# The first graph layer's scan: gate product moved from VectorE to GpSimd, same-row marks in PSUM

## The chip, the cores and the metric

The kernel runs on one core of a Trainium2 chip. The metric is the device time of one execution in microseconds (us), given as the median of several runs. Engines are called as in the profile: PE is TensorE, DVE is VectorE, ACT is ScalarE, POOL is GpSimd, SP is SyncE, the last of which only issues DMAs here. L829 is line 829 of the kernel before.

## What is computed

A graph network of two layers over 6250 nodes of 64 features and 206250 edges, each with a source `src`, a destination `dst`, a type and 32 attributes. The change lies in the first layer, which is this part of the reference:

```python
edge_index = jnp.stack([src, dst])
h = jnp.maximum(_layernorm(x, axis=-1), 0.0)
head = entity_emb[edge_index[0]]                      # entity_emb = h
tail = entity_emb[edge_index[1]]
rel = relation_emb[edge_type]
att_scores = jax.nn.sigmoid(jnp.concatenate([head, rel], axis=-1) @ att_w + att_b)
neighbor_emb = att_scores * tail
aggr_emb = jax.ops.segment_sum(neighbor_emb, edge_index[0], num_segments=N_ENTITIES)
x = x + jnp.tanh(aggr_emb @ W_w.T + W_b)
```

So every edge gives its destination's features times one gate, and the products are summed by source. The second layer is an attention over the same edges, and its result goes through a linear map and is added to `x`.

## The kernel before, in words

Everything runs on one core, in stages one after the other; a stage is an `nc.Block()` (item 1 below has two) in which each engine has its own program, and the engines meet only by semaphores.

1. `setup` and `histogram` load the inputs, normalise the nodes and count the edges of each source.
2. `sort` writes a record of 100 floats for each edge (32 attributes, destination, source, gate, a pad, and the destination's 64 features) into an HBM table in the order of the sources, by scatters from POOL.
3. `relation_layer` is the first layer's scan, the stage of the change.
4. `relation_nodes` takes the running sums at the last edge of each source, and computes the node update and the tables for the second layer.
5. `attention_layer` is the second layer's scan. For each chunk POOL issues 26 gathers (L1126) and DVE does products (L1254, L1256, L1274, L1277), a reduce (L1257) and scans (L1241, L1286).
6. `attention_nodes` writes the result.

The sorted records are cut so that each of the 128 partitions holds a run of 1612 consecutive records. `relation_layer` walks these runs in 62 chunks of T = 26 records per partition, 31 turns of a loop with two halves (b = 0 and 1, buffers of the same number); chunk n = 2i + b. `loop` writes the first and last turn out and loops over the 29 between. The sums by source are made by one scan over the 64 features x 27 places of a chunk, state = keep x state + add: `keep` is 1 where a record has the same source as the one before it, and `add` is the gated features. Place 0 of each feature holds the sum carried over from the chunk before, with keep 0.

Per chunk the engines do this:

- **SP** (L753) loads `rec_r` with the records, 1300 KB, into one of two buffers, once the product two chunks back is done (`s_add`).
- **DVE** prepares (`prepare`, L809 to L812): three small copies out of the records (destination as index, destination, source) and a compare of neighbouring sources into `same`, all 26 wide. Then `scan`: the carry copy (L822), the gate product (L823: features transposed to feature-major times the gate, 1664 elements, into the one buffer `add_r`), and the scan (L829, 1728 elements).
- **ACT** spreads `same` over the 64 features into `keep_r` (L778), copies the scan's result back to record order into `packed_r` (L790) and issues its store (L792, 832 KB).
- **POOL** does nothing here. There is a second way for unsorted extremes (`gather` true, chosen at run time by the flag `k.slow`), in which POOL gathers the destinations' features (L766). In this input the flag is 0, and the trace has no instruction on `got_r`.

The order of the work is the order of each engine's program as written; DVE prepares chunk n right before its product when nothing is gathered:

```python
for b in range(2):
    n = 2 * i + b
    if not gather:
        prepare(n, i, b)
    elif not at_end(i, b):
        prepare(n + 1, i + b, 1 - b)
    scan(n, i, b, gather)
```

Of the kernel before, what the change touches and what calls it, by code (L numbers as in the profile page):

```python
# [22 lines left out]
P = 128  # L23
N, D, E, EC = 6250, 64, 206250, 32
# [6 lines left out]
T = 26  # L31
# [8 lines left out]
T1 = T + 1  # L40
# [29 lines left out]
def bc(ap, dim, n):  # L70

    a = ap.unsqueeze(dim)
    shape = list(a.shape)
    shape[dim] = n
    return a.broadcast_to(shape)


def wait(eng, s, n):

    if not isinstance(n, int) or n > 0:  # L80
        eng.wait_ge(s, n)


def loop(eng, body):


    body(0)
    with eng.Fori(1, PAIRS - 1) as i:
        body(i)
    body(PAIRS - 1)  # L90
# [54 lines left out]
def at_start(i, b=0):  # L145
    return isinstance(i, int) and i == 0 and b == 0


def at_end(i, b=1):
    return isinstance(i, int) and i == PAIRS - 1 and b == 1  # L150
# [568 lines left out]
def relation_layer(k):  # L719


    nc = k.nc
    with ExitStack() as ctx:
        tile, bank, sem = helpers(k, ctx)
        rows = tile("rows", [P, 1 + NT])
        rec = [tile(f"rec_r{b}", [P, T, REC]) for b in range(2)]
        idx = [tile(f"idx_r{b}", [P, T], I32) for b in range(2)]
        got = [tile(f"got_r{b}", [P, T, D]) for b in range(2)]

        keep = [tile(f"keep_r{b}", [P, D, T1]) for b in range(2)]  # L730
        add = tile("add_r", [P, D, T1])
        state = [tile(f"state_r{b}", [P, D, T1]) for b in range(2)]
        packed = [tile(f"packed_r{b}", [P, T, D]) for b in range(2)]
        s_zero, s_idx, s_add, s_state, s_keep, s_packed, s_dve, s_passed = (
            sem(n) for n in ("s_zero_r", "s_idx_r", "s_add_r", "s_state_r", "s_keep_r", "s_packed_r", "s_dve_r", "s_passed_r"))
        s_rec, s_got, s_store = ([sem(f"{n}{b}") for b in range(2)] for n in ("s_rec_r", "s_got_r", "s_store_r"))
        records_v, sums_v = by_run(k.records), by_run(k.sums0)

        def either(eng, body):

            flag = eng.value_load(k.slow[0:1, 0:1], min_val=0, max_val=CHUNKS)
            with eng.If(flag != 0):
                body(True)
            with eng.Else():
                body(False)

        with nc.Block() as block:  # L747
            @block.sync
            def _(sp):
                def body(i):  # L750
                    for b in range(2):
                        wait(sp, s_add, 2 * i + b - 1)
                        sp.dma_start(rec[b][:], records_v[:, bass.ds(i * 2 * T + b * T, T), :]).then_inc(s_rec[b], 16)  # L753

                loop(sp, body)

            @block.gpsimd
            def _(pool):
                def body(i):
                    for b in range(2):  # L760
                        n = 2 * i + b
                        wait(pool, s_add, n - 1)
                        pool.wait_ge(s_idx, n + 1)
                        pool.sem_inc(s_passed, 1)
                        for t in range(T):
                            nc.gpsimd.indirect_dma_start(  # L766
                                got[b][:, t, :], None, k.h_table,
                                bass.IndirectOffsetOnAxis(ap=idx[b][:, t:t + 1], axis=0)).then_inc(s_got[b], 16)

                either(pool, lambda gather: loop(pool, body) if gather else pool.sem_inc(s_passed, 1))  # L770

            @block.scalar
            def _(act):
                def mark(n, i, b):

                    act.wait_ge(s_idx, n + 1)
                    wait(act, s_state, n - 1)
                    nc.scalar.copy(keep[b][:, :, 1:T1], bc(k.same[:, bass.ds(n * T, T)], 1, D)).then_inc(s_keep, 1)  # L778

                act.wait_ge(s_zero, 4)  # L780
                mark(0, 0, 0)

                def body(i):
                    for b in range(2):
                        n = 2 * i + b
                        if not at_end(i, b):
                            mark(n + 1, i + b, 1 - b)
                        act.wait_ge(s_state, n + 1)
                        wait(act, s_store[b], 16 * i)
                        nc.scalar.copy(packed[b][:], state[b][:, :, 1:T1].rearrange("p d t -> p t d")).then_inc(s_packed, 1)  # L790
                        act.wait_ge(s_packed, n + 1)
                        act.dma_start(sums_v[:, bass.ds(n * T, T), :], packed[b][:]).then_inc(s_store[b], 16)  # L792

                loop(act, body)
                for b in range(2):
                    act.wait_ge(s_store[b], 16 * PAIRS)

            @block.vector
            def _(dve):
                c = Chain(dve, s_dve, 2 * 4)  # L800

                def prepare(n, i, b):

                    t0 = i * 2 * T + b * T
                    dve.wait_ge(s_rec[b], 16 * (i + 1))
                    if at_start(i, b):

                        c.mark(nc.vector.tensor_copy(rows[:, 0:1], rec[b][:, 0:1, SRC]))
                    c.mark(nc.vector.tensor_copy(idx[b][:], rec[b][:, :, DST]))  # L809
                    c.mark(nc.vector.tensor_copy(k.dst_s[:, bass.ds(t0, T)], rec[b][:, :, DST]))  # L810
                    c.then(nc.vector.tensor_copy(rows[:, bass.ds(t0 + 1, T)], rec[b][:, :, SRC]))
                    nc.vector.tensor_tensor(k.same[:, bass.ds(t0, T)], rows[:, bass.ds(t0 + 1, T)],  # L812
                                            rows[:, bass.ds(t0, T)], ALU.is_equal).then_inc(s_idx, 1)

                def scan(n, i, b, gather):
                    if gather:
                        dve.wait_ge(s_got[b], SCATTERED * (i + 1))
                    h_dst = got[b][:] if gather else rec[b][:, :, H0:REC]
                    if at_start(i, b):
                        c.mark(nc.vector.memset(add[:, :, 0:1], 0.0))  # L820
                    else:
                        c.mark(nc.vector.tensor_copy(add[:, :, 0:1], state[1 - b][:, :, T:T1]))  # L822
                    nc.vector.tensor_tensor(add[:, :, 1:T1], h_dst.rearrange("p t d -> p d t"),  # L823
                                            bc(rec[b][:, :, GATE], 1, D), ALU.mult).then_inc(s_add, 1)
                    c.wait()
                    dve.wait_ge(s_add, n + 1)
                    dve.wait_ge(s_keep, n + 1)
                    wait(dve, s_packed, n - 1)
                    nc.vector.tensor_tensor_scan(state[b][:].rearrange("p d t -> p (d t)"), keep[b][:].rearrange("p d t -> p (d t)"),  # L829
                                                 add[:].rearrange("p d t -> p (d t)"), 0.0, ALU.mult, ALU.add).then_inc(s_state, 1)  # L830
                    dve.wait_ge(s_state, n + 1)

                for b in range(2):
                    nc.vector.memset(keep[b][:, :, 0:1], 0.0).then_inc(s_zero, 2)

                def way(gather):
                    c.begin(0)
                    c.fewer = 0
                    if gather:
                        prepare(0, 0, 0)  # L840

                    def body(i):
                        if not at_start(i):
                            c.begin(i)
                        for b in range(2):
                            n = 2 * i + b
                            if not gather:
                                prepare(n, i, b)
                            elif not at_end(i, b):
                                prepare(n + 1, i + b, 1 - b)  # L850
                            scan(n, i, b, gather)
                        if not at_end(i):
                            c.end()

                    loop(dve, body)

                either(dve, way)
                c.wait()
                c.mark(nc.vector.tensor_copy(k.first_row[:], rows[:, 1:2]))
                c.mark(nc.vector.tensor_copy(k.last_row[:], rows[:, NT:NT + 1]))  # L860
                c.then(nc.vector.tensor_copy(k.tail0[:], state[1][:, :, T]))
# [785 lines left out]
```

## Time and profile before

| What | Value |
|---|---|
| Median of 3 runs | 7819.6 us (7811.6 to 7821.93) |
| Span of the profiled execution, first to last instruction | 6240.3 us |
| Its own time | the profile gives no other than the span; 1579.3 us below the median |
| Busy in the span | DVE 65%, POOL 67%, PE 39%, ACT 36% |
| Stage of `relation_layer` | 2452.4 to 2962.5 us |

The profile is taken in one execution. "Busy" is time inside instructions; issuing DMAs and waiting for semaphores is not busy. In a group of instructions stand the line, the engine, the operation, output and inputs, the count, the busy time and mean of one, and then the idle time of the engine before them with what ended it. The page's own list of the costliest groups is led by the indirect DMAs of POOL in `attention_layer` and `sort`; the groups of `relation_layer` are found by asking for its stretch of time.

### The profile page before, as it was taken

Reading aid. Unit: us, or ns where it says so; the run is one execution under the profiler, and the core shown is the slowest. Engines: PE = TensorE matmul, PEld = TensorE weight load, DVE = VectorE, ACT = ScalarE, POOL = GpSimd, SP = SyncE. Lnnn points to the kernel's source line nnn. Section 1 sums busy time; section 2 is a strip of 40 time slices with the busy share of each in tenths; the row PEclk is TensorE's granted clock in tenths of the full one; section 3 lists DMA queues with packets and bytes.
Section 4 is the critical chain, followed back from the end, with each engine's and each line's share of the span. In section 5 each row is a group of like instructions: output and inputs, shape, how many; then the busy total and the mean of one; then the engine's idle time right before and its main releaser. Section 6 shows DMA issues by size and latency. Waiting matters only on the chain. (4 is left out here: it accounts for less than half of the span.)

```text
span 6240.3 us, 79656 instructions
## 1 busy us (share of the span) xinstructions
PE 2457.8 (39%) x26472; PEld 2145.9 (34%) x26472; DVE 4084.2 (65%) x6681; ACT 2268.7 (36%) x3099; POOL 4166.8 (67%) x3385
## 2 busy tenths in 40 slices
PE   2877666666666660000632222222222222222215
PEld 2876666666666660000421111111111111111115
DVE  6987777777777773999345655655655655655654
ACT  0033333333333332666244344344344344344332
POOL 0067777777777775000568888888888888888863
PEclk9987777777777775555555555555555555555555
DMA  4022222222222222777133233233233233233211
GB/s 57 18 79 83 74 84 74 84 80 77 83 74 84 74 81 98 271 269 256 39 97 92 81 85 91 80 85 90 80 85 91 80 86 90 80 87 89 80 54 22
DMA packets 459619, 572.09 MB, mean 92 GB/s; under 512 B 349939, under 2 KB 358003, under 8 KB 451632
## 3 DMA queue, kind: packets, MB, share of 16 engines
q1 hardware_dynamic: 309440, 265.27, 15.5%
q0 software_dynamic: 107904, 193.55, 10.9%
q10 hardware_dynamic: 42224, 112.63, 4.7%
q8 instruction: 27, 0.44, 0.0%
q14 instruction: 24, 0.20, 0.0%
HBM read 308.06 MB, written 263.14 MB: 92 GB/s over the span
## 5 line engine op out<-in xcount | busy, mean ns | idle before, releaser
L1126 POOL DMA_INDIRECT got_a<-kv_table,idx_a x1612 | 2390.6, 1483 | 501.1 <-issue 491.0
L497 POOL DMA_INDIRECT records<-rec,place x1612 | 1620.6, 1005 | 824.9 <-issue 491.2
L1254 DVE TENSOR_TENSOR prod<-got_a,query 128x1664 f32<-128x1664 f32 x62 | 188.8, 3046 | 1123.9 <-DMA got_a<-kv_table,idx_a 1123.9
L1140 PE MATMUL p_a<-ident,flat_attr 128*128 128x128 f32 x434 | 108.0, 426 | 1778.2 <-ACT flat_attr L1174 1778.2
L1140 PEld LDWEIGHTS p_a<-ident,flat_attr 128*128 128x128 f32 x434 | 83.5, 221 | 1790.6 <-ACT flat_attr L1174 1790.6
L518 PE MATMUL p_look<-parts,lo_hot_t 128*128 128x98 bf16 x4836 | 503.8, 240 | 129.9 <-DVE earlier L703 129.8
L609 ACT COPY lo_hot_t<-p_t 128x512 bf16<-128x512 bf16 x434 | 241.1, 556 | 711.6 <-PE p_t L542 700.2
L703 DVE TENSOR_TENSOR earlier<-p_same,less_b 128x512 bf16<-128x512 f32 x434 | 282.4, 651 | 274.7 <-PE p_same L564 269.6
L685 DVE TENSOR_SCALAR dst_hot<-p_dst,number 128x512 bf16<-128x512 f32 x434 | 309.0, 712 | 215.1 <-PE p_dst L552 213.8
L518 PEld LDWEIGHTS p_look<-parts,lo_hot_t 128*128 128x128 bf16 x4836 | 397.8, 116 | 140.6 <-DVE earlier L703 140.5
L1198 ACT COPY packed_a<-state_a 128x1768 f32<-128x1768 f32 x62 | 228.0, 3678 | 534.7 <-DVE state_a L1286 534.7
L521 PE MATMUL p_look<-hi_hot,earlier 128*128 128x49 bf16 x1612 | 400.5, 248 | 0.0
L1151 PE MATMUL p_w<-w_t,relu 128*128 128x128 f32 x868 | 261.5, 400 | 352.0 <-ACT soft L1187 352.0
L1151 PEld LDWEIGHTS p_w<-w_t,relu 128*128 128x128 f32 x868 | 214.1, 303 | 421.9 <-ACT soft L1187 421.9
L917 POOL IOTA hi_at_i<- 128x49 int32 x1 | 0.2, 170 | 518.2 <-POOLq L747 518.2
L580 ACT COPY h_dst<-p_h 128x256 f32<-128x256 f32 x434 | 156.1, 360 | 517.4 <-PE p_h L529 514.6
L568 PE MATMUL p_place<-hi_hot,lo_hot 128*128 128x49 bf16 x1612 | 231.0, 274 | 272.7 <-DVE parts L695 272.6
L638 DVE TENSOR_TENSOR picked<-p_look,hi_hot 128x392 f32<-128x392 f32 x434 | 336.6, 776 | 0.0
L1192 ACT ACTIVATE add_a<-below_a 128x104 f32<-128x104 f32 x62 | 18.0, 290 | 781.1 <-DVE below_a L1271 781.1
L564 PE MATMUL p_same<-lo_hot_t 128*128 128x128 bf16 x1612 | 189.3, 247 | 247.0 <-ACT lo_hot_t L609 247.0
L520 PE MATMUL p_look<-hist,lo_hot_t 128*128 128x49 bf16 x2294 | 285.8, 206 | 0.0
L529 PE MATMUL p_h<-window,dst_hot 128*128 128x64 bf16 x4836 | 267.9, 214 | 0.0
(307 smaller groups left out, 8628.9 us busy)
## 6 DMA issues: line engine op xcount, KB each, us to landing
rec_r<-records SPq DMA_DIRECT2D x62, 1300.0 KB, 6.5
sums<-packed_a ACTq DMA_DIRECT2D x62, 936.0 KB, 3.7
q_starts<-zero_q SPq DMA_DIRECT2D x62, 884.0 KB
qin<-q_starts SPq DMA_DIRECT2D x62, 884.0 KB, 6.9
sums<-packed_r ACTq DMA_DIRECT2D x62, 832.0 KB, 6.6
records<-rec,place POOLq DMA_INDIRECT x1612
attr_a<-records SPq DMA_DIRECT2D x62, 416.0 KB, 5.0
got_a<-kv_table,idx_a POOLq DMA_INDIRECT x1612, 2.6
```

What stands on the lines that cost most here:

```text
L497: nc.gpsimd.indirect_dma_start(k.records, bass.IndirectOffsetOnAxis(ap=place[b][:, t:t + 1], axis=0), rec[b][:, t, :], None).then_inc(s_se ...
L518: nc.tensor.matmul(both, at, k.parts[qb][:, part, :, :], start=(part == 0), stop=False)
L520: nc.tensor.matmul(to, at, hist[qb][:, e, :], start=False, stop=False)
L521: last = nc.tensor.matmul(to, earlier[qb][:, j, :], k.hi_hot[b][:, :, g * G + j], start=False, stop=True)
L529: last = nc.tensor.matmul(p_h[:, j * D:(j + 1) * D], dst_hot[qb][:, j * P:(j + 1) * P], window[b][:, part, :], start=(part == 0), stop=(pa ...
L568: last = nc.tensor.matmul(p_place[:, 0:HI], k.lo_hot[b][:, :, t], k.hi_hot[b][:, :, t], start=False, stop=True, skip_group_check=True)
L609: nc.scalar.copy(lo_hot_t[qb][:, 0:size(g) * P], p_t[:, 0:size(g) * P]).then_inc(s_t_copied, 1)
L638: nc.vector.tensor_tensor(picked[:, 0:n, :, :], p_look[gb][:, 0:n * 2 * HI].rearrange("p (g a h) -> p g a h", a=2, h=HI), bc(k.hi_hot[b][: ...
L685: nc.vector.tensor_scalar(dst_hot[qb][:, 0:m * P], p_dst[:, 0:m * P], k.number[:], None, ALU.is_equal).then_inc(s_dst_hot, 1)
L703: nc.vector.tensor_tensor(earlier[qb][:, 0:m, :], p_same[:, 0:m * P].rearrange("p (g e) -> p g e", e=P), bc(k.less_b[:], 1, m), ALU.mult). ...
L1126: nc.gpsimd.indirect_dma_start(got[b][:, t, :], None, k.kv_table, bass.IndirectOffsetOnAxis(ap=idx[b][:, t:t + 1], axis=0)).then_inc(s_got ...
L1151: nc.tensor.matmul(to, relu[:, g * P:(g + 1) * P], k.w2_t[:], start=True, stop=False)
```

## The change

The gate product becomes an instruction of POOL and writes one of two `add_r` buffers. `keep_r` moves from SBUF to PSUM, four banks for each buffer. DVE prepares chunk n + 1 before it scans chunk n in both ways, so it has one loop in place of two. The carry copy gets a semaphore of its own, and SP's load waits also for the compare (`s_idx`) of the chunk two back. POOL's product waits for the records of its chunk and for the scan two chunks back, which read the same `add_r` buffer. What is computed stays the same. The core of the diff:

```diff
-        keep = [tile(f"keep_r{b}", [P, D, T1]) for b in range(2)]
-        add = tile("add_r", [P, D, T1])
+        add = [tile(f"add_r{b}", [P, D, T1]) for b in range(2)]
...
+        keep_flat = [ctx.enter_context(nc.psum_tensor(f"keep_r{b}", [P, 4 * 512], F32))[:, 0:D * T1] for b in range(2)]
+        keep = [flat.rearrange("p (d t) -> p d t", t=T1) for flat in keep_flat]
...
                     for b in range(2):
                         wait(sp, s_add, 2 * i + b - 1)
+                        wait(sp, s_idx, 2 * i + b - 1)
                         sp.dma_start(rec[b][:], records_v[:, bass.ds(i * 2 * T + b * T, T), :]).then_inc(s_rec[b], 16)
...
+                def weigh(n, i, b, gather):
+
+                    pool.wait_ge(s_rec[b], 16 * (i + 1))
+                    if gather:
+                        pool.wait_ge(s_got[b], SCATTERED * (i + 1))
+                    wait(pool, s_state, n - 1)
+                    h_dst = got[b][:] if gather else rec[b][:, :, H0:REC]
+                    nc.gpsimd.tensor_tensor(add[b][:, :, 1:T1], h_dst.rearrange("p t d -> p d t"),
+                                            bc(rec[b][:, :, GATE], 1, D), ALU.mult).then_inc(s_add, 1)
+
+                def way(gather):
+                    if gather:
+                        fetch(0, 0)
+
+                    def body(i):
+                        for b in range(2):
+                            n = 2 * i + b
+                            if gather and not at_end(i, b):
+                                fetch(n + 1, 1 - b)
+                            weigh(n, i, b, gather)
+
+                    loop(pool, body)
+
+                either(pool, way)
...
-                        c.mark(nc.vector.tensor_copy(add[:, :, 0:1], state[1 - b][:, :, T:T1]))
-                    nc.vector.tensor_tensor(add[:, :, 1:T1], h_dst.rearrange("p t d -> p d t"),
-                                            bc(rec[b][:, :, GATE], 1, D), ALU.mult).then_inc(s_add, 1)
-                    c.wait()
+                        nc.vector.tensor_copy(add[b][:, :, 0:1], state[1 - b][:, :, T:T1]).then_inc(s_carry, 1)
+                    dve.wait_ge(s_carry, n + 1)
                     dve.wait_ge(s_add, n + 1)
                     dve.wait_ge(s_keep, n + 1)
                     wait(dve, s_packed, n - 1)
-                    nc.vector.tensor_tensor_scan(state[b][:].rearrange("p d t -> p (d t)"), keep[b][:].rearrange("p d t -> p (d t)"),
-                                                 add[:].rearrange("p d t -> p (d t)"), 0.0, ALU.mult, ALU.add).then_inc(s_state, 1)
+                    nc.vector.tensor_tensor_scan(state[b][:].rearrange("p d t -> p (d t)"), keep_flat[b],
+                                                 add[b][:].rearrange("p d t -> p (d t)"), 0.0, ALU.mult, ALU.add).then_inc(s_state, 1)
                     dve.wait_ge(s_state, n + 1)
...
+                c.begin(0)
+                prepare(0, 0, 0)
+
+                def body(i):
+                    if not at_start(i):
+                        c.begin(i)
+                    for b in range(2):
+                        n = 2 * i + b
+                        if not at_end(i, b):
+                            prepare(n + 1, i + b, 1 - b)
+                        scan(n, i, b)
+                    if not at_end(i):
+                        c.end()
+
+                loop(dve, body)
```

How this moves instructions is seen on DVE and POOL. First DVE in the changed kernel, the first half of a turn of the loop in `relation_layer` (`same` is the compare of chunk n + 1, the copy into `add_r` is the carry of chunk n, `SCALAR_TENSOR_TENSOR` is the scan of chunk n; `ISA` and `REGISTER_ALU` rows are loop counting and waits):

```order
L832 CAST idx_r<-rec_r 128x26 [waits s_rec_r1]
L833 ISA
L833 COPY dst_s<-rec_r 128x26
L834 ISA
L834 COPY rows<-rec_r 128x26
L108 ISA
L835 ISA [waits s_dve_r]
L835 TENSOR_TENSOR same<-rows 128x26
L842 COPY add_r<-state_r 128x64
L843 REGISTER_ALU
L81 REGISTER_ALU [waits s_keep_r,s_add_r,s_carry_r]
L847 SCALAR_TENSOR_TENSOR state_r<-keep_r,add_r 128x1728 [waits s_packed_r]
```

Before, the product stood between the carry copy and the scan, on DVE; now the preparing of the next chunk, the carry copy and the scan follow one another, and the scan waits for POOL (`s_add_r`).

Then POOL in the changed kernel, the way without gathers in `relation_layer`, which before held one branch and no work (first turn, loop, last turn):

```order
L777 TENSOR_TENSOR add_r<-rec_r 128x64x26 [waits s_rec_r0]
L777 TENSOR_TENSOR add_r<-rec_r 128x64x26 [waits s_rec_r1]
L88 UNCONDITIONAL_BRANCH
L88 ISA
L81 ISA [waits s_rec_r0]
L777 TENSOR_TENSOR add_r<-rec_r 128x64x26 [waits s_state_r]
L777 TENSOR_TENSOR add_r<-rec_r 128x64x26 [waits s_state_r,s_rec_r1]
L88 REGISTER_ALU
L88 COMPARE_AND_BRANCH
L777 TENSOR_TENSOR add_r<-rec_r 128x64x26 [waits s_state_r,s_rec_r0]
L777 TENSOR_TENSOR add_r<-rec_r 128x64x26 [waits s_state_r,s_rec_r1]
```

The first two products wait for their records alone; each later one waits for its records and for the scan of two chunks before.

## Rows read from the trace of the kernel before

**Rows 1.** The page's head: the span, then busy time and share per engine.

```profile
span 6240.3 us, 79656 instructions
...
PE 2457.8 (39%) x26472; PEld 2145.9 (34%) x26472; DVE 4084.2 (65%) x6681; ACT 2268.7 (36%) x3099; POOL 4166.8 (67%) x3385
```

**Rows 2.** Busy time of each engine in the stage, then clock, DMA share, GB/s.

```profile
2452.40:2962.50 510.10, 0.00 (x0) 0.00 (x0) 471.55 (x440) 307.49 (x124) 0.00 (x0) 0.50 0.77 264
```

**Rows 3.** Groups of instructions by line in the stage, DVE and ACT.

```profile
L829 DVE TENSOR_TENSOR_SCAN state_r<-keep_r,add_r 128x1728 f32<-128x1728 f32 x62 | 233.0, 3758 | 4.9
...
L823 DVE TENSOR_TENSOR add_r<-rec_r 128x1664 f32<-128x1664 f32 x62 | 196.0, 3162 | 0.0
...
L790 ACT COPY packed_r<-state_r 128x1664 f32<-128x1664 f32 x62 | 215.2, 3471 | 2.1 <-DVE state_r L829 2.1
L778 ACT COPY keep_r<-same 128x1664 f32 (+1 forms) x62 | 98.1, 1582 | 266.1 <-DVE same L812 266.1
```

**Rows 4.** Timeline of DVE over one chunk: start us, us, instruction, idle before.

```profile
2481.44 0.18 DVE L809 CAST idx_r<-rec_r 128x26 int32<-128x26 f32 x1
...
2481.70 0.18 DVE L811 COPY rows<-rec_r 128x26 f32 x1
2482.03 0.19 DVE L812 TENSOR_TENSOR same<-rows  x1
2482.13 0.22 DVE L822 COPY add_r<-state_r 128x64 f32<-128x64 f32 x1
...
2485.45 3.76 DVE L829 TENSOR_TENSOR_SCAN state_r<-keep_r,add_r 128x1728 f32<-128x1728 f32 x1
2489.77 0.18 DVE L809 CAST idx_r<-rec_r 128x26 int32<-128x26 f32 x1 [0.56 <-DVE state_r L829]
```

**Rows 5.** Timeline of DVE: the first and the last index copy.

```profile
2458.16 0.17 DVE L809 CAST idx_r<-rec_r 128x26 int32<-128x26 f32 x1
...
2950.94 0.18 DVE L809 CAST idx_r<-rec_r 128x26 int32<-128x26 f32 x1
```

**Rows 6.** DMA from 2452 to 2965: SP's queue, and the loads' time to landing.

```profile
q1 hardware_dynamic: 8928, 82.54, 52.2%
...
rec_r<-records SPq DMA_DIRECT2D x62, 1300.0 KB, 6.5
```

**Rows 7.** Timeline of POOL at the program's start.

```profile
0.30 0.10 POOL L1638 MEMSET const-float32-0.0<- 128x1 f32 x1 [0.30 <-issue]
...
1.81 0.29 POOL L273 TENSOR_SCALAR_AFFINE_SELECT ident<-ident 128x128 f32<-128x128 f32 x1 [0.16 <-POOL ones L271]
```

**Rows 8.** Groups of DVE over the whole span: one PSUM input, dense SBUF inputs.

```profile
L703 DVE TENSOR_TENSOR earlier<-p_same,less_b 128x512 bf16<-128x512 f32 x434 | 282.4, 651 | 274.7 <-PE p_same L564 269.6 <-issue 0.2
...
L128 DVE TENSOR_TENSOR big<-h 128x3136 f32<-128x3136 f32 x1 | 3.4, 3425 | 0.0
```

**Rows 9.** Timeline: POOL's gathers beside DVE, in `relation_nodes` and `attention_layer`.

```profile
2970.90 6.69 DVE L1029 TENSOR_TENSOR own<-iota_p,own_at 128x6272 f32<-128x6272 f32 x1
2971.87 6.53 POOL L920 DMA_INDIRECT sums_n<-sums,last_at  x1 [0.30 <-issue]
...
4003.80 3.70 DVE L1274 TENSOR_TENSOR got_a<-got_a,net 128x1664 f32<-128x1664 f32 x1
...
4005.01 3.24 POOL L1126 DMA_INDIRECT got_a<-kv_table,idx_a  x1 [0.30 <-issue]
...
4007.60 3.00 DVE L1277 TENSOR_TENSOR add_a<-got_a,add_a 128x1664 f32<-128x1664 f32 x1
...
4010.87 3.98 DVE L1286 TENSOR_TENSOR_SCAN state_a<-scale,add_a 128x1836 f32<-128x1836 f32 x1
4011.69 3.92 POOL L1126 DMA_INDIRECT got_a<-kv_table,idx_a  x1 [0.30 <-issue]
...
4045.70 3.25 DVE L1257 TENSOR_REDUCE logit_a<-prod 128x104 f32<-128x1664 f32 x1
4046.79 0.94 POOL L1126 DMA_INDIRECT got_a<-kv_table,idx_a  x1 [0.30 <-issue]
```

More of the change, by code:

```diff
@@ L728, in relation_layer @@
         got = [tile(f"got_r{b}", [P, T, D]) for b in range(2)]
-        keep = [tile(f"keep_r{b}", [P, D, T1]) for b in range(2)]
-        add = tile("add_r", [P, D, T1])
+        add = [tile(f"add_r{b}", [P, D, T1]) for b in range(2)]
         state = [tile(f"state_r{b}", [P, D, T1]) for b in range(2)]
         packed = [tile(f"packed_r{b}", [P, T, D]) for b in range(2)]
-        s_zero, s_idx, s_add, s_state, s_keep, s_packed, s_dve, s_passed = (
-            sem(n) for n in ("s_zero_r", "s_idx_r", "s_add_r", "s_state_r", "s_keep_r", "s_packed_r", "s_dve_r", "s_passed_r"))
+        keep_flat = [ctx.enter_context(nc.psum_tensor(f"keep_r{b}", [P, 4 * 512], F32))[:, 0:D * T1] for b in range(2)]
+        keep = [flat.rearrange("p (d t) -> p d t", t=T1) for flat in keep_flat]
+        s_zero, s_idx, s_add, s_carry, s_state, s_keep, s_packed, s_dve, s_passed = (
+            sem(n) for n in ("s_zero_r", "s_idx_r", "s_add_r", "s_carry_r", "s_state_r", "s_keep_r", "s_packed_r", "s_dve_r", "s_passed_r"))
         s_rec, s_got, s_store = ([sem(f"{n}{b}") for b in range(2)] for n in ("s_rec_r", "s_got_r", "s_store_r"))
@@ L758, in _, with fetch @@
             def _(pool):
[L759 to L770, printed above, removed]
+                def fetch(n, b):
+                    wait(pool, s_add, n - 1)
+                    pool.wait_ge(s_idx, n + 1)
+                    pool.sem_inc(s_passed, 1)
+                    for t in range(T):
+                        nc.gpsimd.indirect_dma_start(
+                            got[b][:, t, :], None, k.h_table,
+                            bass.IndirectOffsetOnAxis(ap=idx[b][:, t:t + 1], axis=0)).then_inc(s_got[b], 16)
+                def weigh(n, i, b, gather):
[17 more added lines that the diff above has]
+                either(pool, way)
             @block.scalar
@@ L799, in _ @@
             def _(dve):
-                c = Chain(dve, s_dve, 2 * 4)
+                c = Chain(dve, s_dve, 2 * 3)
                 def prepare(n, i, b):
@@ L813, in prepare, with scan @@
                                             rows[:, bass.ds(t0, T)], ALU.is_equal).then_inc(s_idx, 1)
[L815 to L818, printed above, removed]
+                def scan(n, i, b):
                     if at_start(i, b):
-                        c.mark(nc.vector.memset(add[:, :, 0:1], 0.0))
+                        nc.vector.memset(add[b][:, :, 0:1], 0.0).then_inc(s_carry, 1)
                     else:
-                        c.mark(nc.vector.tensor_copy(add[:, :, 0:1], state[1 - b][:, :, T:T1]))
-                    nc.vector.tensor_tensor(add[:, :, 1:T1], h_dst.rearrange("p t d -> p d t"),
-                                            bc(rec[b][:, :, GATE], 1, D), ALU.mult).then_inc(s_add, 1)
-                    c.wait()
+                        nc.vector.tensor_copy(add[b][:, :, 0:1], state[1 - b][:, :, T:T1]).then_inc(s_carry, 1)
+                    dve.wait_ge(s_carry, n + 1)
                     dve.wait_ge(s_add, n + 1)
@@ L834, in _ @@
                     nc.vector.memset(keep[b][:, :, 0:1], 0.0).then_inc(s_zero, 2)
[L836 to L857, printed above, removed]
+                c.begin(0)
[11 more added lines that the diff above has]
+                loop(dve, body)
                 c.wait()
```

## The prediction

> **What bounds the kernel now.** I went from the whole to the stage, then to one chunk. The page's first lines say that no engine is full over the span: DVE 65%, POOL 67%, DMA light [rows 1]. So the change must be priced in its own stage. The table by stage gives the first layer's scan 510.1 us, with DVE busy 471.55 of them, ACT 307.49, POOL nothing, and the DMA engines busy 0.77 of the time [rows 2]. The groups of DVE there show why: 62 chunks, each a product of 3162 ns and a scan of 3758 ns, and, in the timeline, five small instructions of 0.18 to 0.22 us [rows 3, 4]. They stand end to end, with holes of 0.03 to 0.56 us between chunks [rows 4]. From the first index copy at 2458.16 to the last at 2950.94 are 61 chunks, so a chunk takes 8.08 us [rows 5]. The idle time in the groups agrees: ACT sat 266.1 us until DVE's compare [rows 3]. DVE alone sets the pace. Behind it stand the DMA engines: 0.77 x 510.1 / 62 = 6.34 us per chunk.
>
> **The change, part by part.** The sum is against the profiled execution, whose span is 6240.3 us; the median of the runs, 7819.6, is 1579.3 us more. I take what lies around the span as unchanged and add the difference in the stage to the median.
>
> *The product leaves DVE.* Gone: 62 x 3.16 = 196 us of DVE. What stays per chunk is 8.08 - 3.16 = 4.92 us: four instructions of preparing, the carry copy, the scan, the gaps.
>
> *The product arrives on POOL,* and no row has such an instruction. Its price P is bounded by rows. From below: POOL's select over 128 elements takes 0.29 us, and a one-element fill 0.10 [rows 7], so 1.5 ns an element with one input read, or 2.6 us for 1664. With two inputs read in turn the same slope gives 5.0 us. From above: both inputs here are strided by a record of 400 bytes. DVE needs 1.8 ns an element for this product ((3162 - 150) / 1664) and 1.04 for a dense one (3425 ns for 3136, [rows 8]), a surcharge of 0.76 ns; added to 5.0 it gives 6.3. ACT's strided copy takes 3471 ns [rows 3]; two such streams, less one fixed part, are 6.6. I take P = 5.6, between POOL's own slope and the surcharge, and keep 2.6 to 6.6. The Trainium skill, "GPSIMD Engine Reference", section 3.1, states 4497 ns for a GpSimd add of 2048 elements; in proportion that is an estimate of 3.65 us here, and by its section 7 (steps over 8 bytes cost about half again) 5.5 us.
>
> *Does it run beside DVE?* This decides the sign. The rows show a lock in one direction. DVE's product of two SBUF inputs of 6.69 us at 2970.90 stretched POOL's gather at 2971.87 to 6.53 us, that is until 0.8 us after DVE's end. In the second layer the gather at 4011.69 lasted 3.92 us, again until 0.8 us after a two-input scan; the one at 4046.79, under a reduce with one input, took 0.94 [rows 9]. The scan with its marks in PSUM has one SBUF input, like that reduce, so I let it run beside POOL. But preparing still has a compare of two SBUF inputs, `same`, and it stands before the scan in every chunk. Note also the gather of 4005.01: it ended at 4008.25, though the next two-input product had begun at 4007.60, 0.1 us after the first, so POOL got in between the two [rows 9]. Now the order. POOL's product of chunk n+1 and DVE's preparing of n+1 wait for the same two things, the load of n+1 and the end of scan n-1. They start together. POOL reacts in 0.16 us [rows 7]; preparing and carry take from 2481.44 to 2482.35, 0.9 us, with a hole before `same` [rows 4]. POOL gets in. If the lock holds the other way too, DVE's compare then stands until the product ends, the carry and scan n stand behind it, and POOL may not start n+2 before scan n is done, as it writes the buffer that this scan reads. So they alternate:
>
> chunk = 4.92 (DVE) + 0.15 (POOL's reaction) + 5.6 (P) = 10.67 us; change = 62 x (10.67 - 8.08) = +161 us.
>
> The reverse direction is not in these rows, since no POOL instruction there reads SBUF for long. The Trainium skill, "SBUF — State Buffer", "Who interferes with whom", states it: such a pair excludes each other for the whole instruction, and issue order decides who blocks. By that rule the sum stands; without it, it is the first rival's.
>
> *Marks in PSUM.* ACT's copy of 1582 ns may change by some 0.1 us either way; ACT has 8.08 - 3.47 - 1.58 = 3.0 us to spare per chunk [rows 3]. The scan takes (3758 - 158) / 1728 = 2.08 ns an element; DVE's product with one PSUM input takes 651 ns for 512 [rows 8], about 1 ns an element, so I expect no loss. If the read were added it would be 1.8 us x 62 = 111 us more; that far end I hold for unlikely.
>
> *Preparing ahead* only shifts the same instructions, except at the start: `same` of chunk 1 now precedes the first scan and waits for the second load. A load costs 52.2% of 513 us / 62 = 4.3 us of the engines [rows 6], so it lands that much after the first, past the 3.16 us of the first product; with the compare behind it, +2 us. SP's added wait for s_idx is for a compare that lies before the scan of the product it waits for anyway: nothing. If POOL is late, SP's loads are late by the same; at 10.67 us a load of 6.5 us [rows 6] is hidden.
>
> Sum: 161 + 2 = 163; 7819.6 + 163 = **7983 us**.
>
> **The rivals.**
>
> *1. No exclusion against the small instructions (faster).* Then POOL's product lies under the scan. Candidates per chunk: POOL 5.75; DVE 4.92; ACT 5.05 and its DMA issue; the buffer ring (6.5 landing + 5.6 + 0.3) / 2 = 6.2; DMA 6.34. I take 6.5: 62 x (6.5 - 8.08) = -98, so 7722 us. For it: no row shows POOL holding DVE. Against: the lock seen from the other side. It decides wherever DVE's compare and copies pass while POOL reads.
>
> *2. DVE often wins the race.* After a chunk whose preparing is through before POOL begins, the product hides. Half the chunks each way: (10.67 + 6.5) / 2 = 8.6, +32 us, 7852. Against it: POOL's 0.16 us against 0.9 us of preparing.
>
> *3. Excluded, but the product is short.* Break-even is P = 3.16 - 0.15 = 3.0 us; at the low bound of 2.6 the change gives 62 x (2.6 - 3.0) = -25, 7795. That needs the second input to be free.
>
> *4. Side by side, but POOL is the bound.* If P were 10 us, outside my bounds, the chunk is 10.2 and the time 7950.
>
> **How the numbers follow.** Alternation 0.53, rival 1 0.31, rival 2 0.09, rival 3 0.03, rival 4 0.04. The likeliest gives 7983, and alone, for P of 4.3 to 6.6, it gives 7900 to 8045. A measurement of this kernel tells about 0.2%, 16 us, from no change. Faster: rival 1 but for a slow product (0.29), and the fast ends of rivals 2 and 3 (0.04): 0.33. Same: the middle of rival 2 (0.04) and the alternation with P near 3 (0.02): 0.06. Slower: the rest, 0.61. The range must reach rival 1 at 7722; I take 7715 to 8045.
>
> **What would show it.** Right: in the stage of the first scan, POOL busy for some 62 x 5.6 = 350 us; the stage about 670 us long; on DVE the compare `same`, or the copy before it, stretched or begun late by 5 us in each chunk, and no overlap of POOL's product with it; the DMA share down to 0.58; the scan still 3758 ns. Wrong: small instructions at 0.18 us while POOL's product runs and a stage near 415 us with a DMA share of 0.95 (rival 1); a POOL product under 3 us; a scan longer than 3.9 us; or a stage whose chunks differ in length in turn (rival 2). Other stages should keep their length.

## The result, and the profile after

The changed kernel takes 7998.7 us (median of 4 runs, 7993.0 to 8001.29) against 7820.8 us before (4 runs, 7811.6 to 7825.84). The ratio is 1.0228, with a 95% interval of 1.0214 to 1.0243: 178 us slower, where +163 was forecast.

First a correction that the reading of all numbers needs. The profile of the kernel before has a span of 6240.3 us, the one of the changed kernel 7991.1. The difference is not the change. In the view by stages, up to the scan's stage 2452 us passed in the one and 3937 in the other, with the same code. The kernel before, profiled once more (the first experiment), took 6239.34 us with a span of 6237.4, so only 2 us lie around a span. I had put the 1579 us between span and median around the span. They lie in the stages before the scan, where the two traces differ by 1484 us, and for 90 us behind it. So I compare medians only within one set of runs, and in the traces the stage itself, from the first load of `rec_r` to the first instruction of the next stage. That stage was 513.6 us in both profiles of the kernel before, and is 690.2 us in the changed one: +176.6 us, all of the difference.

The stage of the changed kernel, busy time of each engine, then clock, DMA share and GB/s (it answers to [rows 2]):

```profile
3936.80:4627.00 690.20, 0.00 (x0) 0.00 (x0) 648.99 (x378) 312.38 (x124) 390.78 (x63) 0.50 0.52 196
```

DVE is "busy" for 648.99 us, though it lost 196 us of work. What that is shows in the groups by line, busy and mean, then idle before with its releaser ([rows 3]):

```profile
L777 POOL TENSOR_TENSOR add_r<-rec_r 128x1664 f32<-128x1664 f32 x62 | 390.8, 6303 | 288.2 <-DVE state_r L847 277.7 <-DMA rec_r<-records 10.5
L832 DVE CAST idx_r<-rec_r 128x26 int32<-128x26 f32 x62 | 359.7, 5802 | 15.8 <-DVE state_r L847 11.9
L847 DVE TENSOR_TENSOR_SCAN state_r<-keep_r,add_r 128x1728 f32<-128x1728 f32 x62 | 232.9, 3757 | 4.7
...
L801 ACT COPY keep_r<-same 128x1664 f32 (+1 forms) x62 | 96.1, 1550 | 269.1 <-DVE same L835 269.1
L833 DVE CAST dst_s<-rec_r 128x26 f32 (+1 forms) x62 | 28.7, 463 | 0.0
L835 DVE TENSOR_TENSOR same<-rows (+1 forms) x62 | 17.5, 282 | 8.2
```

The index copy of 26 numbers, 182 ns before, now has a mean of 5802 ns. The product on POOL takes 6303 ns, and POOL sat idle 277.7 us until scans had ended. The timeline over two chunks shows how these fit ([rows 4]; start, us, instruction, idle before):

```profile
3999.30 3.76 DVE L847 TENSOR_TENSOR_SCAN state_r<-keep_r,add_r 128x1728 f32<-128x1728 f32 x1
4003.14 6.31 POOL L777 TENSOR_TENSOR add_r<-rec_r 128x1664 f32<-128x1664 f32 x1 [4.66 <-DVE state_r L847]
...
4003.19 6.29 DVE L832 CAST idx_r<-rec_r 128x26 int32<-128x26 f32 x1
...
4009.40 0.17 DVE L833 CAST dst_s<-rec_r 128x26 f32 x1
4009.49 0.17 DVE L834 COPY rows<-rec_r 128x26 f32 x1
4009.80 0.19 DVE L835 TENSOR_TENSOR same<-rows  x1
4009.91 0.22 DVE L842 COPY add_r<-state_r 128x64 f32<-128x64 f32 x1
...
4010.16 3.76 DVE L847 TENSOR_TENSOR_SCAN state_r<-keep_r,add_r 128x1728 f32<-128x1728 f32 x1
```

The scan ends, POOL's product starts first by 0.05 us, DVE's index copy starts and stands until the product is over, then the other small instructions run at their usual 0.17 to 0.22 us, and the scan follows. Product and scan alternate: in the whole stage no scan overlaps a product. The first chunks show that it isn't a matter of this one copy. There POOL came later into the row, and the compare and the next copy were held instead:

```profile
3942.67 12.58 POOL L777 TENSOR_TENSOR add_r<-rec_r 128x1664 f32<-128x1664 f32 x2 [10.48 <-DMA rec_r<-records]
3942.70 0.17 DVE L834 COPY rows<-rec_r 128x26 f32<-128x26 f32 x1
3942.91 6.13 DVE L835 TENSOR_TENSOR same<-rows 128x26 f32<-128x26 f32 x1
...
3949.05 6.24 DVE L833 CAST dst_s<-rec_r 128x26 int32<-128x26 f32 x1
...
3955.77 3.76 DVE L847 TENSOR_TENSOR_SCAN state_r<-keep_r,add_r 128x1728 f32<-128x1728 f32 x1
```

Of the 60 later products, 58 hold the index copy, for 6.05 to 6.31 us. In the two others the index copy started up to 0.05 us before the product and took 0.18 us, and the copy after it was held instead. So it did not help DVE to be first with a small instruction.

From the first index copy at 3942.52 to the last at 4604.87 are 61 chunks of 10.86 us ([rows 5]: 8.08). Forecast was 10.67.

### The profile page after: what moved, and what is told of

The parts are those of the page before. It is cut to its first block and busy times, and to the rows that moved or that the text cites. A ratio compares the mean times of both kernels' runs of the same rounds, so it can differ in the third digit from the quotient of the medians.

```text
span 7991.1 us, 79829 instructions
## 1 busy us (share of the span) xinstructions
PE 2703.3 (34%) x26472; PEld 2243.8 (28%) x26472; DVE 4265.7 (53%) x6619; ACT 2274.5 (28%) x3099; POOL 4496.2 (56%) x3447
## 5 line engine op out<-in xcount | busy, mean ns | idle before, releaser
L497 POOL DMA_INDIRECT records<-rec,place x1612 | 1558.0, 966 | 2371.9 <-ACTq L599 1887.7
L518 PE MATMUL p_look<-parts,lo_hot_t 128*128 128x98 bf16 x4836 | 528.3, 249 | 417.2 <-DVE earlier L703 407.1
L529 PE MATMUL p_h<-window,dst_hot 128*128 128x64 bf16 x4836 | 369.2, 218 | 576.0 <-issue 576.0
L777 POOL TENSOR_TENSOR add_r<-rec_r 128x1664 f32<-128x1664 f32 x62 | 390.8, 6303 | 288.2 <-DVE state_r L847 277.7
L529 PEld LDWEIGHTS p_h<-window,dst_hot 128*128 128x128 bf16 x4836 | 273.9, 114 | 589.5 <-issue 589.5
L568 PE MATMUL p_place<-hi_hot,lo_hot 128*128 128x49 bf16 x1612 | 255.8, 273 | 440.6 <-issue 227.7
L564 PE MATMUL p_same<-lo_hot_t 128*128 128x128 bf16 x1612 | 233.3, 256 | 435.3 <-issue 435.1
L832 DVE CAST idx_r<-rec_r 128x26 int32<-128x26 f32 x62 | 359.7, 5802 | 15.8 <-DVE state_r L847 11.9
```

The source lines that it names most:

```text
L497: nc.gpsimd.indirect_dma_start(k.records, bass.IndirectOffsetOnAxis(ap=place[b][:, t:t + 1], axis=0), rec[b][:, t, :], None).then_inc(s_se ...
L518: nc.tensor.matmul(both, at, k.parts[qb][:, part, :, :], start=(part == 0), stop=False)
L529: last = nc.tensor.matmul(p_h[:, j * D:(j + 1) * D], dst_hot[qb][:, j * P:(j + 1) * P], window[b][:, part, :], start=(part == 0), stop=(pa ...
L568: last = nc.tensor.matmul(p_place[:, 0:HI], k.lo_hot[b][:, :, t], k.hi_hot[b][:, :, t], start=False, stop=True, skip_group_check=True)
L777: nc.gpsimd.tensor_tensor(add[b][:, :, 1:T1], h_dst.rearrange("p t d -> p d t"), bc(rec[b][:, :, GATE], 1, D), ALU.mult).then_inc(s_add, 1)
```

## The experiments

The theory, called exclusion below: while POOL's product reads SBUF, DVE's small copies and its compare cannot run; the scan is free of it only because its marks are in PSUM, and with the marks in SBUF product and scan would hold each other. The rivals: the two engines run side by side and the loss lies in the later order of work (preparing ahead); PSUM; or the product's length alone. "Chunk" below is the time between the first and the last index copy over 61.

**The kernel before, again.**

> The kernel before, unchanged, for a second profile: its first one has a span 1579 us under the median, the changed kernel's has one of 7991. Expected: a span near 7818 us, with the difference in the sorting stage, and the first layer's scan stage again 513 us long (8.08 us a chunk). If the difference lay around the span, the span would be 6240 again.

6239.34 us, span 6237.4, stage 513.7, chunk 8.08. The stage is as long as expected. The span is not near 7818, as I had expected: time and span agree within 2 us, and the whole run took the short time. In another set of runs, with experiments of its own below, the kernel before took 7853.5 us. Below, each kernel is compared with the kernel before as run in the same set. Variants of both kernels appear at either level, so the two levels, short and long, are not of the kernel, and the scan's stage keeps its length: 513.6 us here, and 512.5 at the long level with the marks alone moved to PSUM. Each set of runs was on one chip: the short level was seen on chips 0 and 3, the long one on chip 12, and for the first result the chip is not known. In the profile of the changed kernel PE sat idle 576.0 us before the matmuls of L529 with no releaser that the profile shows ("issue"), in the first profile of the kernel before 0.0. Whether the chip sets the level, or something else, wasn't tried.

**The product's start moved behind the small instructions.**

```diff
-                    wait(pool, s_state, n - 1)
+                    wait(pool, s_carry, n)
```

> Changed kernel, but POOL's product of chunk n+1 waits for the carry copy of chunk n instead of the scan of n-1, so it starts when DVE has its small instructions behind it and begins scan n. Exclusion theory: product and scan overlap, DVE's next index copy is held only from the scan's end to the product's end, 2.5 us; a chunk is 6.30 (product) + 0.7 (small instructions) + 0.1 = 7.1 us; 7820 - 62 x (8.08 - 7.1) = 7759 us, faster than both. Rival, the exclusion also holds between the product and the scan (marks in PSUM do not help): 6.3 + 3.8 + 0.9 = 11 us a chunk, 8000 us. Rival, a later start is only a later start (no exclusion at all): the product ends later and the time is not below the changed kernel's 7999.

6207.88 us against 6241.78 for the kernel before, ratio 0.9945 (0.9928 to 0.9962). With this one wait changed, the kernel is 34 us faster than the kernel before, and by the stages (476.5 against 690.2) 214 us faster than the changed kernel. Chunk 7.41 us. The timeline shows the product beside the scan, each at its own length:

```profile
2601.16 0.22 DVE L842 COPY add_r<-state_r 128x64 f32<-128x64 f32 x1
...
2601.46 6.29 POOL L777 TENSOR_TENSOR add_r<-rec_r 128x1664 f32<-128x1664 f32 x1 [1.35 <-DVE add_r L842]
2601.50 3.76 DVE L847 TENSOR_TENSOR_SCAN state_r<-keep_r,add_r 128x1728 f32<-128x1728 f32 x1
...
2607.35 0.44 DVE L832 CAST idx_r<-rec_r 128x26 int32<-128x26 f32 x1 [2.09 <-DMA rec_r<-records]
```

So the product does not stop a scan with one SBUF input, and both rivals in that text fall. The gain is 34 and not 61 us since another wait ended last: DVE's index copies waited for loads (the row gives us in total, times and the longest). A load begins when its buffer's product is over and took 7.4 us to land (median), and preparing and the next product of that buffer stand behind it: 6.3 + 7.4 + 0.8 + 0.3 = 14.8 us for two chunks, which fits the measured 7.41 a chunk.

```profile
DVE idx_r L832 <- DMA rec_r<-records: 157.3, 60, 3.1
```

**The marks back in SBUF.**

```diff
-        keep_flat = [ctx.enter_context(nc.psum_tensor(f"keep_r{b}", [P, 4 * 512], F32))[:, 0:D * T1] for b in range(2)]
-        keep = [flat.rearrange("p (d t) -> p d t", t=T1) for flat in keep_flat]
+        keep = [tile(f"keep_r{b}", [P, D, T1]) for b in range(2)]
+        keep_flat = [k_[:].rearrange("p d t -> p (d t)") for k_ in keep]
```

> Changed kernel with the same-row marks back in SBUF, so the scan has two SBUF inputs. Exclusion theory: product and scan never overlap in the changed kernel, so nothing changes: 10.9 us a chunk, 7999 us within 5. Rival, reading PSUM costs or saves the scan time: the scan's 3757 ns changes and the time by 62 times that.

6421.52 us, 180 us above the kernel before of the same runs (the changed kernel: 178 above its own), chunk 10.85, scan 3758 ns:

```profile
L847 DVE TENSOR_TENSOR_SCAN state_r<-keep_r,add_r 128x1728 f32<-128x1728 f32 x62 | 233.0, 3758 | 4.7
```

The difference is the expected one. In the changed kernel the move to PSUM bought nothing, since product and scan never meet.

**Both edits.**

> Both edits: product starts with the scan, and the scan has two SBUF inputs. Exclusion theory: now product and scan exclude each other; a chunk is 6.3 + 3.8 + 0.8 = 10.9 us, about 7995 us, and one of the two instructions is stretched by the other in the profile. Rival, the scan does not take part in the exclusion, whatever its inputs: like the run with the gate alone, 7759 us.

6412.92 us, 171 above the kernel before (175 expected), chunk 10.62. This and the run with the gate differ in the memory of the marks alone, by 205 us. The timeline shows the exclusion in both directions between two long instructions:

```profile
2596.33 6.27 POOL L777 TENSOR_TENSOR add_r<-rec_r 128x1664 f32<-128x1664 f32 x1 [0.77 <-DVE add_r L842]
2596.38 9.84 DVE L847 TENSOR_TENSOR_SCAN state_r<-keep_r,add_r 128x1728 f32<-128x1728 f32 x1
...
2607.31 3.76 DVE L847 TENSOR_TENSOR_SCAN state_r<-keep_r,add_r 128x1728 f32<-128x1728 f32 x1
2607.36 9.81 POOL L777 TENSOR_TENSOR add_r<-rec_r 128x1664 f32<-128x1664 f32 x1 [4.76 <-DVE add_r L842]
```

Whichever is first by 0.05 us keeps its own length; the other is stretched by about that length. In the stage 31 of the 62 products and 30 of the 62 scans are stretched. The lock is shown from both sides.

**Not preparing ahead.**

```diff
-                        if not at_end(i, b):
-                            prepare(n + 1, i + b, 1 - b)
+                        prepare(n, i, b)
                         scan(n, i, b)
```

> Changed kernel, but DVE prepares chunk n right before scan n instead of one chunk ahead. The small instructions stay as many and are held by POOL's product as before, so the exclusion theory keeps the 10.86 us a chunk; but now ACT spreads the marks of chunk n (1.55 us) between the compare and scan n, with only the carry copy (0.2) beside it: 12.3 us a chunk, 62 x 4.2 = 262 us above the kernel before. Rival, preparing ahead is what costs (it makes the small instructions meet the product): then without it the chunk falls to 8 or below and the time to the kernel before's.

8109.07 us against 7853.49, ratio 1.0327 (1.031 to 1.0344): 256 us above (262 expected), chunk 12.52. The scans waited for ACT's marks, 60 times, 1.8 us each, and the chunk is 1.7 us longer than 10.86:

```profile
ACT keep_r L801: 106.4, 60
```

Preparing ahead is not the cause of the loss but spares that much. The held instruction changes with the moment at which POOL starts; here even the carry copy was held:

```profile
4096.91 6.33 POOL L777 TENSOR_TENSOR add_r<-rec_r 128x1664 f32<-128x1664 f32 x1 [6.82 <-DMA rec_r<-records]
4097.01 6.32 DVE L842 COPY add_r<-state_r 128x64 f32<-128x64 f32 x1
```

**The product back on DVE, the rest of the change kept.**

```diff
-                either(pool, way)
+                pool.sem_inc(s_passed, 1)
...
+                    nc.vector.tensor_tensor(add[b][:, :, 1:T1], rec[b][:, :, H0:REC].rearrange("p t d -> p d t"),
+                                            bc(rec[b][:, :, GATE], 1, D), ALU.mult).then_inc(s_add, 1)
                     dve.wait_ge(s_carry, n + 1)
```

> Changed kernel with the product back on DVE, in front of the scan (two add buffers, marks in PSUM, preparing ahead stay). No product on POOL, so no exclusion: no stretched instruction. Exclusion theory alone: 8.08 us a chunk, as the kernel before. But the load of n+1 starts only when product n-1 is done, and preparing n+1 now stands before product n: landing 6.5 + small 0.8 + product 3.2 = 10.5 us a chunk, 150 us above the kernel before, with DVE waiting for the load. So I expect the second; if it is level with before, the ring of buffers does not matter.

7962.37 us, 109 above (ratio 1.0144, 1.0127 to 1.0161), chunk 9.72. No instruction is stretched, yet it is slower than before: preparing ahead puts the wait for load n+1 in front of product n. I had expected 150 with a landing of 6.5 us; it was 5.7 here, and 5.7 + 0.8 + 3.1 = 9.6 us fits the chunk.

```profile
DVE idx_r L831 <- DMA rec_r<-records: 121.7, 61, 2.4
```

**Only the marks in PSUM,** the kernel before otherwise.

> Kernel before with the marks alone moved to PSUM. Expected: the same time within 5 us, scan 3757 ns, ACT's spreading 1550 ns and off the path. Rival: PSUM reading slows DVE's scan, +1 ns an element, 111 us.

7853.56 us against 7853.49, ratio 1.0000 (0.9991 to 1.001). The scan takes 3757 ns with a PSUM input and 3758 without, ACT's spreading 1551 and 1582 ns. The move is free.

**Dense inputs for POOL's product.**

```diff
-                    nc.gpsimd.tensor_tensor(add[b][:, :, 1:T1], h_dst.rearrange("p t d -> p d t"),
-                                            bc(rec[b][:, :, GATE], 1, D), ALU.mult).then_inc(s_add, 1)
+                    flat = rec[b][:].rearrange("p t c -> p (t c)")
+                    nc.gpsimd.tensor_tensor(add[b][:, :, 1:T1], flat[:, 0:D * T].rearrange("p (d t) -> p d t", t=T),
+                                            flat[:, 900:900 + D * T].rearrange("p (d t) -> p d t", t=T), ALU.mult).then_inc(s_add, 1)
```

> Changed kernel, but POOL's product reads two dense stretches of the record tile instead of the strided features and gate (the gating is replaced by other numbers, so the output is not the reference's). It measures how much of the 6.30 us is the stride. The Trainium skill, GPSIMD Engine Reference, section 3.1, by its 4497 ns for 2048 elements would give an estimate of 3.65 us; the slope of the select would give 5.0. Exclusion theory: the time falls by 62 times what the product gets shorter, one for one, since nothing runs beside it: at 3.7 us by 161 us, to about 18 us above the kernel before; at 5.0 by 81. Rival, the product's length is partly hidden: the time falls by less than 62 times the difference.

This kernel leaves the gating out: it multiplies other numbers, and only its time counts. The product takes 3.71 us, 2.59 less, and the chunk 8.26, 2.60 less than 10.86: one for one, as exclusion wants. The stride is thus 41% of the product. The time is 7852.55 us, level with the kernel before (ratio 0.9998, 0.9988 to 1.0007), where 18 us above it were expected. The stage, 529.4 us, is still 16 us longer than 513.6. In the trace the scan's stage starts 13 us earlier than in the run with the marks alone. At this level that start lay anywhere from 3937 to 3973 us, so the total is a poor measure of 16 us in the stage, and why it came out level stays open. The held copy has the product's new length:

```profile
4105.06 3.70 POOL L778 TENSOR_TENSOR add_r<-rec_r 128x1664 f32<-128x1664 f32 x1 [4.64 <-DVE state_r L848]
4105.11 3.69 DVE L833 CAST idx_r<-rec_r 128x26 int32<-128x26 f32 x1
```

**A version that beats both.** From the kernel before, with two `add_r` buffers and the marks in PSUM; POOL multiplies half of the features of chunk n+1, started by DVE's own half of chunk n, that is together with scan n.

```diff
+                def weigh(n, i, b, gather):
...
+                    wait(pool, s_add, n)
+                    h_dst = got[b][:] if gather else rec[b][:, :, H0:REC]
+                    nc.gpsimd.tensor_tensor(add[b][:, 0:SPLIT, 1:T1], h_dst[:, :, 0:SPLIT].rearrange("p t d -> p d t"),
+                                            bc(rec[b][:, :, GATE], 1, SPLIT), ALU.mult).then_inc(s_part, 1)
...
-                    nc.vector.tensor_tensor(add[:, :, 1:T1], h_dst.rearrange("p t d -> p d t"),
-                                            bc(rec[b][:, :, GATE], 1, D), ALU.mult).then_inc(s_add, 1)
+                    nc.vector.tensor_tensor(add[b][:, SPLIT:D, 1:T1], h_dst[:, :, SPLIT:D].rearrange("p t d -> p d t"),
+                                            bc(rec[b][:, :, GATE], 1, D - SPLIT), ALU.mult).then_inc(s_add, 1)
```

> A version meant to beat both: from the kernel before, with marks in PSUM and two add buffers, half of the 64 features of chunk n+1 are multiplied on POOL, started when DVE has finished its own half of chunk n and begins scan n; DVE prepares chunk n right before its half. Exclusion theory: POOL's half takes about 3.2 us and lies wholly under the scan of 3.76, so no DVE instruction is held; DVE per chunk 4.92 + 1.65 = 6.6 us, near the DMA engines' 6.34: 62 x (8.08 - 6.6) = 92 us below the kernel before if the loads land in time, about 60 if they hold a part (landing took 7.4 us in the run with the gate). Rival, any POOL product beside DVE's scan costs DVE its length: no gain over the kernel before.

6178.21 us against 6252.94, ratio 0.9881 (0.9865 to 0.9898): 75 us faster, chunk 6.81, DMA share 0.85 in 2460 to 2860. POOL's half ends before the scan does. In the loop no DVE instruction is held; only the compare of the very first chunk is, at 2461.18, for 3.05 us beside POOL's first half. A chunk of the loop:

```profile
2613.11 1.64 DVE L848 TENSOR_TENSOR add_r<-rec_r 128x832 f32<-128x832 f32 x1
...
2614.83 3.23 POOL L779 TENSOR_TENSOR add_r<-rec_r 128x832 f32<-128x832 f32 x1 [3.80 <-DVE add_r L848]
2614.95 3.76 DVE L855 TENSOR_TENSOR_SCAN state_r<-keep_r,add_r 128x1728 f32<-128x1728 f32 x1 [0.20 <-DVE add_r L848]
```

It is 75 and not 92 us: the chunk is 0.2 us longer than expected, 13 us in all. Of these 8.1 are the scans' waits for ACT's marks, in 30 chunks; with a shorter product on DVE, the marks have less cover. Where the rest lies was not worked out.

```profile
DVE state_r L855 <- ACT keep_r L803: 8.1, 30, 0.5
```

> The same with 26 features on POOL and 38 on DVE: POOL's part 2.6 us, over a microsecond before the scan's end, DVE 4.92 + 1.95 = 6.9 us a chunk. If POOL's end in the run with 32 collides with the next preparing, this one is faster; if DVE's length sets the chunk, it is slower by 62 x 0.3 = 19 us.

6185.54 us, ratio 0.9888 (0.9872 to 0.9905), chunk 6.93; POOL's part takes 2652 ns. By the chunk 0.12 us slower, 7 us in all, less than the 19 expected. It has its expected length of 6.9 us, with the marks covered again (0.2 us of waits); the run with 32 was the longer one. The intervals of the two ratios overlap, so which share is better is open.

## Why the prediction was right

By its own steps:

- *What bounds the kernel:* right. DVE set the pace. The run with half the product on POOL took 1.27 us off each chunk, by taking 1.5 us of DVE's work away.
- *The sign, by exclusion:* right, and shown by three comparisons: the gate, the gate with and without PSUM, and the dense product. The Trainium skill's "SBUF — State Buffer", "Who interferes with whom", was the only source for the direction from POOL to DVE before the result; the traces now agree, with 6.13 us for a compare of 0.19.
- *The instruction that is held:* partly wrong. My step went by the number of SBUF inputs and named the compare, with the copy before it as a second possibility. It is mostly the index copy, the first of the row: POOL was ready 0.05 us earlier than DVE, and copies with one SBUF input are held too (6.29 us for 0.18), while the scan with one SBUF input is not. What sets the copies apart from the scan no run shows.
- *The sum:* it puts all of DVE's 4.92 us in series with the product. That fits the index copy being held, and not my own step: with only the compare held, the copies before it would pass beside the product, and they are 0.6 us of the chunk (2481.44 to 2482.03 in [rows 4]). By that step a chunk should have been 10.67 - 0.59 = 10.08 us, which is +124 us for the 62 chunks in place of +161. So it was luck that the sum fits the real order.
- *P = 5.6 us:* mis-sized, it is 6.30; that is 43 us over 62 chunks. The Trainium skill's "GPSIMD Engine Reference", section 3.1, gave an estimate of 3.65 us for dense inputs, and 3.71 was measured. By its section 7 a step over 8 bytes adds half; here, with both inputs strided, it added 70%.
- *DVE's part and POOL's reaction, 4.92 + 0.15:* they measured 10.86 - 6.30 = 4.56 us. POOL started before DVE's copy could, and the first hole and the copy itself lie inside the product. That takes 32 us back. So the terms of the chunks add up to 161 + 43 - 32 = 172 us, where two errors of opposite sign nearly cancel; that 163 comes so near to 178 is partly luck. The break-even of the product was put at 3.0 us; by the chunk of the dense run it is 8.08 - 4.55 = 3.5.
- *Marks in PSUM, nothing:* right.
- *Preparing ahead, +2 us:* the size is near, the reason wrong. I had expected the second load to come late; but POOL went through its first two products without a hole, and the first scan waited for both. It began 19.0 us into the stage, before 9.4, where one product stood ahead of it (the row below). The stage gained 9.6 us up to its first scan and 167 us from there to the last one, 176.6 in all, which is some 4 us more than 172. DVE stands still in this kernel anyway; with the product on DVE the same order costs 109 us.

```profile
2461.87 3.76 DVE L829 TENSOR_TENSOR_SCAN state_r<-keep_r,add_r 128x1728 f32<-128x1728 f32 x1
```

- *The rivals:* no exclusion, DVE winning the race, a product under 3 us and a product of 10 us each fell at one row. The stage is 690 and not 670 us by the longer product. The DMA share is 0.52 and not 0.58, and the longer stage explains only 0.57: the DMA engines' busy time itself fell, from 0.77 x 510 = 393 us to 0.52 x 690 = 359. Why was not looked into.
- *What lies around the span:* wrong, as told above, without effect on the difference.

## What to carry to other kernels

Moving an instruction with SBUF inputs from DVE to POOL frees DVE only while DVE's own instructions stay off the path that the two share. One small copy in between is enough to make the engines take turns, and a profile shows it as a tiny instruction with the other engine's length. One SBUF input is not enough to be safe: the scan with one passed, the copies with one were held, so look in the profile for which of them keep their length. Start POOL's instruction together with a DVE instruction that is seen to pass beside it and that is longer than it, and size the share to fit. And when a step is prepared ahead, look at what it waits for and what now stands behind that wait.

## What the runs showed of the hardware that I had not expected

- An instruction that reads two dense fp32 inputs on POOL took 2.23 ns an element (3.71 us for 1664), with both inputs at a step of 400 bytes 3.79 ns (6.30 us). The parts of 832 and 676 elements took 3.23 and 2.65 us, so the slope is 3.7 ns and there is little fixed cost.
- DVE's scan takes 3757 ns for 1728 elements, whether its marks are read from SBUF or PSUM.
- The stages before the scan took 2449 to 2456 us in some sets of runs and 3937 to 3973 us in others, with the same code. The change touches none of them.
